# Last four experts of the last block in pairs of token tiles, the mean of y taken off by ScalarE

## The reference, cut to what matters

```python
x = x + layernorm(memory(layernorm(x)))      # memory: one gradient step on a two-layer net, then a query of it
x = x + layernorm(ffn(layernorm(x)))         # this half is where the change lies

def ffn(x):                                  # E = 8 experts, TOP_K = 2, H = 128, HF = 256
    z = layernorm(x) * g + b
    probs = softmax(z @ rW + rb)             # the two best experts of a token get the weights w, summing to 1
    hid = gelu(einsum("bth,ehf->btef", z, W1) + b1)
    outs = einsum("btef,efh->bteh", hid, W2) + b2
    return x + sum over e of outs[..., e, :] * w[..., e]
```

## Time and profile before

| | us |
|---|---|
| median of 3 runs | 188.84 (187.68 to 188.96) |
| the profiled execution's own time | 187.79 |
| its span, first to last instruction | 186.0 |

### The profile page before, as it was taken

One profiled execution on the slowest core, in us unless ns is written; L12 is line 12 of the kernel. 1 busy time (PEld: TensorE's weight loads), 2 busy tenths in 40 slices (PEclk: granted clock), 3 DMA queues, 4 the chain that ended last, 5 costly groups with the idle time before them and its releaser, 6 DMA issues.

```text
span 186.0 us, 3109 instructions
## 1 busy us (share of the span) xinstructions
PE 168.9 (91%) x1036; PEld 136.4 (73%) x1036; DVE 137.1 (74%) x541; ACT 95.4 (51%) x165; POOL 25.2 (14%) x36
## 2 busy tenths in 40 slices
PE   6589999998999798996999999999999999999950
PEld 6334455666655367995999998998999998989940
DVE  0989998997766828399356979866979775458574
ACT  3059776765575597242725435725426725346300
POOL 1450000000031700024000025100026000002011
PEclk9999999999999999999999999999999999999995
DMA  4991000000000000000000000100000100000101
GB/s 140 310 314 42 5 4 0 0 0 2 4 0 0 0 0 2 4 0 0 0 4 0 2 0 4 56 0 0 5 0 0 59 2 0 0 4 2 56 0 56
DMA packets 3423, 4.99 MB, mean 27 GB/s; under 512 B 336, under 2 KB 1744, under 8 KB 3408
## 3 DMA queue, kind: packets, MB, share of 16 engines
q1 hardware_dynamic: 3408, 4.81, 8.2%
HBM read 3.76 MB, written 1.05 MB: 26 GB/s over the span
## 4 chain that ended last, share of the span: by engine, by line
PE 72%; DVE 17%; ACT 3%; issue 2%; DMA 2%; POOL 1%; SPq 0%; DVEq 0%; ACTq 0%
PE bank L372 66%; PE bank L380 4%; DVE stats L831 3%; DMA x_tok<-in_x_dram 2%; DVE xnT L1083 2%; DVE mv L834 1%; DVE xn_tok L988 1%; PE bank L525 1%; DVE xn_tok L844 1%; PE bank L516 1%; DVE h_tok L844 1%; ACT L753 1%; DVE xnT L1094 1%; DVE xnT L1114 1%; DVE xnT L1066 1%
## 5 line engine op out<-in xcount | busy, mean ns | idle before, releaser
L1083 DVE SCALAR_TENSOR_TENSOR xnT<-bank,w_tok,xnT 128x128 f32<-128x128 f32 x124 | 34.9, 345 | 24.4 <-PE bank L372 23.8
L325 POOL TENSOR_TENSOR rstd<-vpe,minus_half 128x4 f32<-128x4 f32 (+1 forms) x24 | 21.8, 913 | 116.5 <-DVE vpe L839 105.3
L372 PE MATMUL bank<-z_hi,fW_hi 128*128 128x512 f32 x64 | 27.8, 434 | 0.3 <-ACT alrT L649 0.3
L372 PE MATMUL bank<-z_hi,fW_lo 128*128 128x512 f32 x64 | 25.0, 390 | 0.0
L372 PE MATMUL bank<-z_lo,fW_hi 128*128 128x512 f32 x64 | 25.0, 393 | 0.0
L372 PEld LDWEIGHTS bank<-fW_sb,sig 128*128 128x128 f32 x192 | 23.0, 192 | 0.7
L372 PE MATMUL bank<-fW_sb,sig 128*128 128x128 f32 x192 | 23.2, 275 | 0.0
L772 ACT ACTIVATE sig<-bank,early_sb 128x512 f32<-128x512 f32 x24 | 16.1, 687 | 10.5 <-PE bank L372 10.4
L372 PEld LDWEIGHTS bank<-fW_sb,k_tok 128*128 128x128 f32 x160 | 19.4, 191 | 0.8
L372 PEld LDWEIGHTS bank<-fW_sb,h1T 128*128 128x128 f32 x160 | 19.4, 191 | 0.8
L372 PE MATMUL bank<-fW_sb,k_tok 128*128 128x128 f32 x160 | 19.5, 275 | 0.0
(11 more groups left out here) (128 smaller groups left out, 266.9 us busy)
## 6 DMA issues: line engine op xcount, KB each, us to landing
x_tok<-in_x_dram SPq DMA_DIRECT2D x4, 256.0 KB, 4.3
fW_raw<-in_fW_dram SPq DMA_DIRECT2D x1, 1024.0 KB, 9.8
out_dram<-xn_tok SPq DMA_DIRECT2D x3, 256.0 KB, 2.5
early_sb<-in_early_dram SPq DMA_DIRECT2D x1, 268.0 KB, 3.8
late_sb<-in_late_dram SPq DMA_DIRECT2D x1, 264.0 KB, 4.7
b_raw<-in_late_dram SPq DMA_DIRECT2D x16, 4.0 KB
out_dram<-xn_tok SPq DMA_DIRECT2D x2, 128.0 KB, 1.9
fW_sb<-in_fW_dram SPq DMA_DIRECT2D x1, 0.5 KB, 12.1
```

The costliest lines, as they stand in the source:

```text
L325: pool.tensor_tensor(rstd[:, ln, where], vpe[:, ln, where], minus_half[:, 0:where.stop - where.start], ALU.pow).then_inc(rstd_ready[ln], 1)
L372: return pe.matmul(out_, lhsT, rhs, start=start, stop=stop)
L1083: last = dve.scalar_tensor_tensor(out=y_tok[:, t, :], in0=bank[Y_BANK[m % len(Y_BANK)]][:, i * P:(i + 1) * P], scalar=w_tok[:, t, e:e + 1] ...
```

## The change

The output products of the last four steps, 28 to 31, are no longer made whole in their slots. `output_pair(k)` makes one of eight products of two token tiles, 8 matmuls each: k = 0 to 3 are tiles 0 and 1 for steps 28 to 31, in slots 28 to 31; k = 4 to 7 are tiles 2 and 3 for the same steps, after them. They go to banks 6, 2, 4, 7 in turn. VectorE adds them in the same order with `add_pair(k)`, two instructions each.

The normalisation of the last block's two parts is done in another way: VectorE writes the negated mean into `neg_mean` (`y_centre`), ScalarE adds it to `y_tok` (two instructions per part, after its last gelu), and VectorE computes x1 + rstd * y_tok in one instruction per tile (`y_last`). The first three blocks keep `y_norm`. VectorE's list now runs `y_last` of part 3 between `add_pair(5)` and `add_pair(6)`.

```diff
...
@@ -233,8 +234,10 @@
 
 
         H_BANK, Y_BANK, B2_BANK = (0, 1, 5), (6, 2), 3
-        LAST_BANK = (4, 7)
+        LAST_BANK = (6, 2, 4, 7)
         HALF = TB // 2
+        LAST = 4
+        WHOLE = STEPS - LAST
 
         AHEAD = 2
         R_SUM, NORM_R, RESIDUAL, NORM_Z, Y_STATS, Y_NORM, Z_LOW, CHOOSE, ROUTE = -1, 0, 1, 2, 2, 3, 4, 5, 6
@@ -600,20 +603,28 @@
 
             def output(m):
 
-                e = m % E
-                into = bank[Y_BANK[m % len(Y_BANK)]]
                 pe.wait_ge(g_done, C * m + C)
                 if m >= len(Y_BANK):
                     pe.wait_ge(acc_done, m - len(Y_BANK) + 1)
-                for i in range(TB):
-                    if m == STEPS - 1:
-                        into = bank[LAST_BANK[i // HALF]]
-                        if i == HALF:
-                            last.then_inc(y_mm, 1)
+                token_tiles(m, bank[Y_BANK[m % len(Y_BANK)]], range(TB))
+
+            def token_tiles(m, into, where):
+                e = m % E
+                for i in where:
                     for c in range(C):
                         last = mm(into[:, i * P:(i + 1) * P], g_buf[(C * m + c) % G_RING][:, i * P:(i + 1) * P],
                                   fW2_sb[:, (e * C + c) * H:(e * C + c + 1) * H], start=(c == 0), stop=(c == C - 1))
                 last.then_inc(y_mm, 1)
+
+            def output_pair(k):
+
+                half, m = k // LAST, WHOLE + k % LAST
+                pe.wait_ge(g_done, C * m + C)
+                if k < len(Y_BANK):
+                    pe.wait_ge(acc_done, WHOLE - len(Y_BANK) + k + 1)
+                elif k >= len(LAST_BANK):
+                    pe.wait_ge(acc_done, WHOLE + k - len(LAST_BANK) + 1)
+                token_tiles(m, bank[LAST_BANK[k % len(LAST_BANK)]], range(half * HALF, half * HALF + HALF))
 
             pe.wait_ge(fw_lo_done, PIECES)
             for slot in range(-AHEAD, STEPS):
@@ -631,8 +642,13 @@
                     b2_term(0)
                 if due(B2_TERM, slot):
                     b2_term(due(B2_TERM, slot))
-                if slot >= 0:
+                if 0 <= slot < WHOLE:
                     output(slot)
+                if slot >= WHOLE:
+                    output_pair(slot - WHOLE)
+                if slot == STEPS - 1:
+                    for k in range(LAST, 2 * LAST):
+                        output_pair(k)
                 if due(R_TR, slot):
                     r_transpose(due(R_TR, slot) + 1)
                 if due(Z_TR, slot):
@@ -796,6 +812,11 @@
                     gate_tanh(due(GATE, slot))
                 if due(W_TR, slot):
                     wT_out(due(W_TR, slot))
+            for q in (NB - 1, NB):
+                act.wait_ge(mean_ready, q - NB + 2)
+                for t in range(part_tiles(q).start, part_tiles(q).stop):
+                    last = act.activation(y_tok[:, t, :], y_tok[:, t, :], ACT.Identity, bias=neg_mean[:, t:t + 1])
+                last.then_inc(y_centred, 1)
 
 
         @block.vector
@@ -1086,14 +1107,15 @@
                                                     op0=ALU.mult, op1=ALU.add)
                 last.then_inc(acc_done, 1)
 
-            def add_last_expert(half):
-                dve.wait_ge(y_mm, STEPS + half)
-                dve.wait_ge(acc_done, STEPS - 1)
+            def add_pair(k):
+                half, m = k // LAST, WHOLE + k % LAST
+                dve.wait_ge(y_mm, WHOLE + k + 1)
+                dve.wait_ge(acc_done, WHOLE if k == LAST else WHOLE + k)
                 for i in range(half * HALF, half * HALF + HALF):
                     t = T - TB + i
                     last = dve.scalar_tensor_tensor(out=y_tok[:, t, :],
-                                                    in0=bank[LAST_BANK[half]][:, i * P:(i + 1) * P],
-                                                    scalar=w_tok[:, t, E - 1:E], in1=y_tok[:, t, :],
+                                                    in0=bank[LAST_BANK[k % len(LAST_BANK)]][:, i * P:(i + 1) * P],
+                                                    scalar=w_tok[:, t, m % E:m % E + 1], in1=y_tok[:, t, :],
                                                     op0=ALU.mult, op1=ALU.add)
                 last.then_inc(acc_done, 1)
 
@@ -1101,9 +1123,25 @@
 
 
                 first, count = PARTS[q]
-                dve.wait_ge(acc_done, (first // TB + 1) * E + (1 if q == NB else 0))
+                dve.wait_ge(acc_done, (first // TB + 1) * E + (LAST if q == NB else 0))
                 yield from statistics(LY, range(first, first + count), lambda i, t: y_tok[:, t, :])
                 plus_eps(LY, part_tiles(q))
+
+            def y_centre(q):
+                where = part_tiles(q)
+                dve.tensor_scalar(neg_mean[:, where], mv[:, LY, where, 0], -1.0, None,
+                                  ALU.mult).then_inc(mean_ready, 1)
+
+            def y_last(q):
+                where = part_tiles(q)
+                dve.wait_ge(y_centred, q - NB + 2)
+                dve.wait_ge(rstd_ready[LY], q + 1)
+                dve.wait_ge(centred, NB)
+                for t in range(where.start, where.stop):
+                    last = dve.scalar_tensor_tensor(out=x1_tok[:, t, :], in0=y_tok[:, t, :],
+                                                    scalar=rstd[:, LY, t:t + 1], in1=x1_tok[:, t, :],
+                                                    op0=ALU.mult, op1=ALU.add)
+                last.then_inc(yn_done, 1)
 
             def y_norm(q):
 
@@ -1135,7 +1173,7 @@
                 if slot >= 0:
                     if slot % E == 0:
                         start_sum(slot // E)
-                    if slot < STEPS - 1:
+                    if slot < WHOLE:
                         add_expert(slot)
                 if due(R_SUM, slot):
                     hidden_sum(due(R_SUM, slot) + 1)
@@ -1156,12 +1194,18 @@
                     run(choose(due(CHOOSE, slot)))
                 if due(ROUTE, slot):
                     run(route(due(ROUTE, slot)))
-            add_last_expert(0)
+            for k in range(LAST):
+                add_pair(k)
             run(y_stats(NB - 1))
-            add_last_expert(1)
+            y_centre(NB - 1)
+            add_pair(LAST)
+            add_pair(LAST + 1)
+            y_last(NB - 1)
+            for k in range(LAST + 2, 2 * LAST):
+                add_pair(k)
             run(y_stats(NB))
-            run(y_norm(NB - 1))
-            run(y_norm(NB))
+            y_centre(NB)
+            y_last(NB)
 
 
 # ---- launch: one core; the small inputs side by side in two arrays, for two transfers ----
```

More of the change, by code:

```diff
@@ L146, in memory_and_experts @@
         neg_shift = sb("neg_shift", [P, T])
+        neg_mean = sb("neg_mean", [P, T])
         minus_half = sb("minus_half", [P, TB])
@@ L190, in memory_and_experts @@
             "shift_ready", "centred", "lg_read", "dp_done"))
-        h_mm, g_done, y_mm, b2_mm, init_done, acc_done, yn_done = (sem(n) for n in (
-            "h_mm", "g_done", "y_mm", "b2_mm", "init_done", "acc_done", "yn_done"))
+        h_mm, g_done, y_mm, b2_mm, init_done, acc_done, yn_done, mean_ready, y_centred = (sem(n) for n in (
+            "h_mm", "g_done", "y_mm", "b2_mm", "init_done", "acc_done", "yn_done", "mean_ready", "y_centred"))
         WAVE = ["dh1", "dz2", "z2", "h1", "n2", "z1", "alr", "gw2", "dz1", "v", "gw1", "k", "n1", "kp", "x", "fw"]
```

## The result

The changed kernel takes 186.80 us, the median of 20 runs (186.59 to 189.37), against 187.89 us for the kernel before, also of 20 runs (187.56 to 190.16). The ratio is 0.9944, 95% interval 0.9923 to 0.9966: by this ratio it is faster by about 1.05 us; the two medians lie 1.09 apart. That is within 1%, as forecast with 0.87, but 186.8 lies under the stated range (187.0 to 188.9), and the gain is larger than the 0.67 us of the forecast and than its band of 0.5 to 0.9. The prediction was wrong in size, not in kind.

The account below looks back on a forecast made before the run. VectorE's queue from 175.58 us on was taken as the bound. Removing 0.66 idle, 0.51 additions, 0.43 and 0.03 normalisation, less 0.66 for y_last and about 0.3 waits, gave 0.67 gain: 188.2 us from median 188.84, range 187.0 to 188.9.

Parts of the forecast that it names:

- its band of 0.5 to 0.9: Whole kernel: the gain in us around the forecast 0.67 that counted as the forecast case, chance 0.60.
- TensorE loses nothing: TensorE from step 28 on: same matmuls, end stays at about 179.12 us; pair 3's gelus ready 0.59 us ahead.
- VectorE up to y_last of part 3: VectorE's list from 175.58 us: negated mean 177.10, additions 4 and 5 until 178.50, y_last of part 3 at 178.55, no idle.
- y_last of part 3 costs 0.66 in the queue: VectorE between additions 5 and 6: two instructions for 0.61 us, with gaps of 0.05 between neighbours.
- The two legs of the end tie: Last part, before the final y_last: GpSimd's rstd lets VectorE start at 182.41 us, ScalarE's centring at 182.42.
- The tail of 2.30 stays: Behind VectorE's end: last output transfer and close of the program keep their 2.30 us, the transfer's size being the same.
- Against the median of 188.84: Whole kernel: the 0.67 us gain set against the earlier median of 188.84 instead of the profiled 187.79, giving 188.2 us.
- the gain did not shrink: Rival at ScalarE's end leg, count waits and y_last's waits: gain only 0.32 or none, 188.5 to 188.8 us; chance 0.20.
- the detour through ScalarE did not stall: Rival at part 3: late centring by ScalarE holds up VectorE's queue, 1.1 us slower, 189.9 us; chance 0.06.
- pair 3 did not wait for its gelus: Rival on TensorE: step 31's gelus late, TensorE idles, VectorE's 175.58 start moves; gain 0.56, 188.3 us; chance 0.05.
- y_last was not cheap: Rival on VectorE: two y_last instructions cost 0.30 us instead of 0.61, gain 1.3, time 187.5 us; chance 0.09.
- the old normalising instruction run faster than one with two tensors: Skill rule weighed against the exchange on VectorE: y_last would cost about 0.07 us a tile more, 0.13 per part.

Follow-up runs that it names:

- The forced count wait: Changed kernel with one more wait: y_last of part 3 waits for the count of addition 5, just ahead on VectorE; 187.04 us (1 run), tail 3.83 against 3.61.

## Why the prediction was right or wrong

*TensorE loses nothing*: right. From step 28's output to the last matmul, 8.67 for 8.68, and pair 3's gelus came in time.

*VectorE up to y_last of part 3*: right to 0.01 us. Counted from step 28's output start, the forecast had the negated mean at 177.10 - 170.44 = 6.66 and the end of addition 5 at 8.06; measured were 6.66 and 8.05.

*y_last of part 3 costs 0.66 in the queue*: the step that failed. It starts at 8.11 in the forecast and at 7.97 in fact, and addition 6 starts at 8.77 in the forecast and at 8.49 in fact. Between additions 5 and 6 lay 0.44 us and not 0.71. The two instructions took 0.60, as forecast; the mistake was the 0.05 us of gap before and behind them. I took it between two rows where an instruction waits for the one ahead of it. These don't wait for it, and such neighbours overlap by 0.08. The forced count wait shows the difference: 0.2 for one such place. The rest of the list kept the error: 12.59 in the forecast, 12.28 measured, so a gain of 0.97 and not 0.67. The trace of before had a place of the same kind, the last additions of step 27 followed by the normalisation of block 2, which doesn't wait for it:

```profile
169.79 0.60 DVE L1083 SCALAR_TENSOR_TENSOR xnT<-bank,w_tok,xnT 128x128 f32<-128x128 f32 x2
170.30 1.11 DVE L1114 TENSOR_SCALAR xnT<-xnT,mv,rstd 128x128 f32<-128x128 f32 x4
```

The first ends at 170.39 and the second starts at 170.30, an overlap of 0.09.

*The two legs of the end tie*: right. With VectorE taking the mean off, y_last started 1.04 us behind the last plus-eps, for 1.03 in the changed kernel.

*The tail of 2.30 stays*: right, 2.35.

*Against the median of 188.84*: this made the larger part of the distance between 188.2 and 186.80. The sum made against the profiled execution was 187.79 - 0.67 = 187.12; I then put it on a median of three, two of which (188.84 and 188.96) lay, by their times, in the group of runs with TensorE's stretch at half clock. The median of 20 was 187.89. Both runs that I had near 187.7 were the ones to build on: 187.79 less the 0.97 measured in the tail is 186.82. The range's floor of 187.0 was made from the right run (187.68) and the too small gain; with 0.97 it would have been 186.7. So that the result fell under the range is the work of the failed step above.

*The rivals*: the gain did not shrink, the detour through ScalarE did not stall (it can, at a price of 0.80 for 1.18 of delay), pair 3 did not wait for its gelus (they ended at 173.82 + 1.24 = 175.06, pair 3 started about 0.85 later), and y_last was not cheap. Nor did the old normalising instruction run faster than one with two tensors: 0.60 for two y_last, 0.60 for two L1114. The plain subtraction of one number per token took 0.48 for two in the kernel where VectorE takes the mean off. The Trainium skill, VectorE: DVE Perf Modes, "The perf-mode tier table", has a float32 tensor_scalar in SBUF at twice the rate of an instruction with two tensors. At 128 columns the traces show at most a fifth less.

**What the 0.97 consists of**: the pairs bring 0.88, the new last part 0.31, and y_last of part 3 standing in the queue costs 0.22 (0.33 in the queue, less the 0.11 that it costs at GpSimd when it stands in the last wait).

## What to carry to other kernels

Where an engine works off a queue behind the last producer, cut the last producers' work so that the queue stays fed and ends just behind them; here the whole change took 0.97 us off the tail with four experts in pairs and 1.34 with six. Cost a queue by whether each instruction waits for the one ahead of it: in these traces 0.03 us of gap where that is its only wait (179.21 to 179.24), 0.10 where it is one of two (178.50 to 178.60) and 0.13 where it is one of four (the forced count), but 0.08 of overlap if it doesn't wait for it. Before adding a gain to a median of a few runs, look at each run's mean clock, or at least whether the times fall into two groups: a second group is not noise around the first.

## What was not expected of the hardware

- TensorE's clock falls back to 1.2 GHz early in some executions of one and the same kernel. In the changed kernel's profile it had been busy 6.0 us with transposes, then idle 1.15, then busy 0.66, then idle 0.78, and fell between 10 and 11 us; in the kernel before, 2.13 and 0.78 of idle in the same places went without a fall. Three of the four falls in the profiles came between 10 and 11 us and lasted 3 to 4 us, the fourth came at about 8.6 and lasted until about 15.4. With these gaps mostly filled none of 13 runs fell (7 and 6), against 12 of 32 and, with six experts, 7 of 12. What tells an execution that falls from one that doesn't was not found. The length of the first 28 transposes doesn't: 5.05 to 6.01 us in the four profiles with the fall, 4.66 to 6.01 in those without. The idle time behind them doesn't either: 1.09 to 1.90 with, 0.73 to 2.58 without.
- GpSimd's 128x2 instruction took 0.80 us beside VectorE instructions with two SBUF tensors (y_last, in three kernels), 0.73 beside the old normalisation, and 0.70 beside additions out of PSUM, partly beside the two subtractions of one tensor, and with VectorE idle. The Trainium skill, GPSIMD Engine Reference, names such contention in its specifications. The traces agree, with 0.1 us for it.
